# Graph layers on one core: one buffer per layer for the summed messages in place of two, every accumulating scatter behind the landing of the one before it

## The reference

```python
def _gin_layer(x, ei, ea, p, concat):
    enc_w, enc_b, w1, b1, g, be, rm, rv, w2, b2 = p
    ee = ea @ enc_w + enc_b
    src = x[ei[1]]
    h = jnp.concatenate([src, ee], axis=1) if concat else src + ee
    agg = jax.ops.segment_sum(h, ei[0], num_segments=x.shape[0])
    h = agg @ w1 + b1
    h = jax.nn.relu(_bn_eval(h, g, be, rm, rv))
    return h @ w2 + b2
```

## Time and profile before

| what | value |
|---|---|
| median of 3 runs | 15496.48 us (15484.17 to 15514.05) |
| span of the profiled execution, first to last instruction | 13500.7 us |
| the profiled execution's own time | not given apart from its span |
| busy, share of the span | PE 56%, weight loads 40%, DVE 47%, ACT 31%, POOL 55% |
| mean granted clock of TensorE | 0.730 |
| gathers L637 | 784 of one form, 811.0 us, 1034 ns each (392 more read the first layer's input) |
| scatters L649 | 1176, 1847.8 us, 1571 ns each |
| adds of the two buffers L1341 | 588, 417.0 us, 713 ns each |
| loads of the sum buffers L435 | 1176, of 256 KB (784) and 290 KB (392) |
| stores of zeros L398 | 1182, of 256 KB (788) and 290 KB (394) |
| read from and written to HBM | 882.49 and 989.71 MB |

### The profile page before, as it was taken

How to read it: one execution, slowest core, us unless ns; L and a number is a source line. 1 busy time by engine, 2 the same in 40 slices (tenths; PEclk the granted TensorE clock), 3 DMA queues, 4 the chain that set the end, 5 groups by cost and what they waited for, 6 DMA issues and landing times.

```text
span 13500.7 us, 178567 instructions
## 1 busy us (share of the span) xinstructions
PE 7584.9 (56%) x35409; PEld 5358.3 (40%) x35409; DVE 6400.1 (47%) x28822; ACT 4190.8 (31%) x8872; POOL 7379.7 (55%) x6837
## 2 busy tenths in 40 slices
PE   6777555555555555554222488842228993222888
PEld 3333444434444333433212355631225662222565
DVE  6777666667666677775222344411113331111444
ACT  7999311111111222221000255510004550000443
POOL 4444677777777777777777400057770007776000
PEclk9999666666666666665555799965559995555999
DMA  6777931138111652222333455533226772223988
GB/s 230 265 266 266 347 131 46 46 104 293 47 47 47 219 208 69 69 69 57 45 45 45 110 192 196 195 70 40 40 40 207 232 231 41 40 40 57 273 268 259
DMA packets 1765076, 1853.43 MB, mean 137 GB/s; under 512 B 232093, under 2 KB 1250168, under 8 KB 1764794
## 3 DMA queue, kind: packets, MB, share of 16 engines
q1 hardware_dynamic: 1424418, 1430.53, 32.1%
q0 software_dynamic: 332416, 418.41, 15.4%
q10 hardware_dynamic: 7960, 2.01, 0.1%
HBM read 882.49 MB, written 989.71 MB: 139 GB/s over the span
## 4 chain that ended last, share of the span: by engine, by line
issue 16%; POOL 11%; DMA 10%; PE 8%; SPq 5%; DVE 3%; POOLq 1%; DVEq 0%; ACT 0%; ACTq 0%
DMA bXd<-agg_d 8%; POOL bO L637 6%; POOL agg_d L649 5%; PE ps L991 3%; SPq L435 2%; PE ps L978 2%; DMA agg_d<-dO,dOI 2%; SPq L433 2%; DVE aO L1368 1%; PE ps L968 1%; DVE bXd L1341 1%; PE ps L940 1%; PE ps L979 1%; DVE eE L1362 1%; SPq L438 0%
## 5 line engine op out<-in xcount | busy, mean ns | idle before, releaser
L637 POOL DMA_INDIRECT bO<-g_d,dGI x784 | 811.0, 1034 | 2486.2 <-DMA g_d<-aH 2242.2
L649 POOL DMA_INDIRECT agg_d<-dO,dOI x1176 | 1847.8, 1571 | 473.8 <-issue 376.2
L949 PE MATMUL ps<-bO,bNE 128*128 128x128 f32 (+1 forms) x2352 | 836.0, 470 | 1569.4 <-DMA bO<-g_d,dGI 1040.7
L767 ACT COPY dO<-ps 128x128 f32<-128x128 f32 (+1 forms) x1176 | 319.3, 272 | 3550.6 <-DMA agg_d<-dO,dOI 3497.6
L949 PEld LDWEIGHTS ps<-bO,bNE 128*128 128x128 f32 x2352 | 563.7, 305 | 1825.0 <-issue 1793.3
L978 PE MATMUL ps<-aS,W1X 128*128 128x512 f32 x2352 | 1207.9, 594 | 5.8 <-DMA eET<-eaT_d 5.3
L991 PE MATMUL ps<-W,aT 128*128 128x128 f32 x9408 | 1133.4, 280 | 27.9 <-ACT aS L784 27.9
L891 PE MATMUL ps<-ident,bSB 128*128 128x128 f32 x1176 | 288.0, 425 | 1522.6 <-DVE bSB L1194 1522.6
L991 PEld LDWEIGHTS ps<-W,aT 128*128 128x128 f32 x9408 | 1102.3, 196 | 48.0 <-ACT aS L784 46.8
L790 ACT ACTIVATE aT<-ps,BNT,BNS 128x512 f32<-128x512 f32 x1176 | 911.2, 775 | 654.2 <-PE ps L979 628.0
L1376 DVE TENSOR_TENSOR aH<-ps,B 128x512 f32<-128x512 f32 x588 | 406.7, 692 | 1252.2 <-PE ps L991 1252.2
(11 more groups left out here) (188 smaller groups left out, 19624.4 us busy)
## 6 DMA issues: line engine op xcount, KB each, us to landing
agg_d<-zeros SPq DMA_DIRECT2D x788, 256.0 KB
bXd<-agg_d SPq DMA_DIRECT2D x784, 256.0 KB, 4.4
agg_d<-zeros SPq DMA_DIRECT2D x394, 290.0 KB
bXd<-agg_d SPq DMA_DIRECT2D x392, 290.0 KB, 4.1
yg_d<-aYG SPq DMA_DIRECT2D x196, 512.0 KB, 3.0
aX<-yg_d SPq DMA_DIRECT2D x392, 256.0 KB, 4.0
g_d<-aH SPq DMA_DIRECT2D x392, 256.0 KB, 3.7
aX<-g_d SPq DMA_DIRECT2D x392, 256.0 KB, 3.8
```

The source lines that it names most:

```text
L637: pool.indirect_dma_start(dG[:, u, 0:C], None, gin_in[m], bass.IndirectOffsetOnAxis(ap=dGI[:, u:u + 1], axis=0), bounds_check=lim2 if m == ...
L649: pool.indirect_dma_start(agg_d[m][u % 2], bass.IndirectOffsetOnAxis(ap=dOI[:, u:u + 1], axis=0), dO[:, u, 0:AW[m]], None, bounds_check=ag ...
L949: pe.matmul(ps[2 + u % 4][:, 0:AW[m]], dS[:, u, :], dG[:, u, 0:AW[m]], start=True, stop=True).then_inc(d_acc, 1)
```

## The change

Each layer keeps one sum buffer. All scatters go to it and count up one semaphore `d_a`; each waits until all scatters ahead of it have landed. SP clears one buffer per layer, loads one in the dense stage, and VectorE reads it directly. The target of e_in's count falls from 48 to 32.

```diff
-    agg_d = [[dram(f"agg{m}{b}_d", (NR, AW[m])) for b in range(2)] for m in range(M)]
+    agg_d = [dram(f"agg{m}_d", (NR, AW[m])) for m in range(M)]
...
             for m in range(M):
-                for b in range(2):
-                    agg = agg_d[m][b]
-                    n = J * AW[m]
-                    sp.wait_ge(b_fm, m * R + 1)
-                    with sp.Fori(0, NT + 1) as i:
-                        sp.dma_start(agg[bass.ds(i * TN, TN), :].rearrange("(p j) c -> p (j c)", j=J),
-                                     zeros[:, 0:n]).then_inc(s_zero, 16)
+                n = J * AW[m]
+                sp.wait_ge(b_fm, m * R + 1)
+                with sp.Fori(0, NT + 1) as i:
+                    sp.dma_start(agg_d[m][bass.ds(i * TN, TN), :].rearrange("(p j) c -> p (j c)", j=J),
+                                 zeros[:, 0:n]).then_inc(s_zero, 16)
...
-                    for b in range(2):
-                        sp.dma_start(eA[:, k, b, :, 0:AW[m]], pick(agg_d[m][b])).then_inc(e_in[k], 16)
+                    sp.dma_start(eA[:, k, :, 0:AW[m]], pick(agg_d[m])).then_inc(e_in[k], 16)
...
                     pool.wait_ge(d_o, U * r + u + 1)
-                    if not isinstance(r, int) or U * r + u >= 2:
-                        pool.wait_ge(d_a[u % 2], 16 * ((U // 2) * r + u // 2))
+                    if not isinstance(r, int) or U * r + u >= 1:
+                        pool.wait_ge(d_a, 16 * (U * r + u))
                     pool.sem_inc(s_gate, 1)
-                    pool.indirect_dma_start(agg_d[m][u % 2],
+                    pool.indirect_dma_start(agg_d[m],
                                             bass.IndirectOffsetOnAxis(ap=dOI[:, u:u + 1], axis=0),
                                             dO[:, u, 0:AW[m]], None, bounds_check=agg_last,
-                                            oob_is_err=True, compute_op=ALU.add).then_inc(d_a[u % 2], 16)
+                                            oob_is_err=True, compute_op=ALU.add).then_inc(d_a, 16)
...
                         if not isinstance(r, int) or r > 0:
-                            act.wait_ge(d_a[u % 2], 16 * ((U // 2) * (r - 1) + u // 2 + 1))
+                            act.wait_ge(d_a, 16 * (U * (r - 1) + u + 1))
                         act.copy(dO[:, u, 0:AW[m]], ps[2 + u % 4][:, 0:AW[m]]).then_inc(d_o, 1)
...
                 def add_up(p, m=m, n0=n0):
-                    for k in range(2):
-                        v.wait_ge(e_in[k], 48 * (m * NA + p + 1))
-                        v.tensor_tensor(eA[:, k, 0, :, 0:AW[m]], eA[:, k, 0, :, 0:AW[m]], eA[:, k, 1, :, 0:AW[m]],
-                                        ALU.add).then_inc(e_a, 1)
                     if m == 0:
-                        v.wait_ge(e_a, 2 * p + 2)
+                        for k in range(2):
+                            v.wait_ge(e_in[k], 32 * (p + 1))
...
                     for k in range(2):
-                        v.wait_ge(e_a, n0 + 2 * p + k + 1)
+                        v.wait_ge(e_in[k], 32 * (m * NA + p + 1))
                         if not isinstance(p, int):
                             v.wait_ge(e_tp, n0 + 2 * p + k - 1)
-                        v.tensor_tensor(eS[:, k, :, :], eA[:, k, 0, :, 0:C], eG[:, k, :, :], ALU.add
+                        v.tensor_tensor(eS[:, k, :, :], eA[:, k, :, 0:C], eG[:, k, :, :], ALU.add
                                         ).then_inc(e_s, 1)
```

More of the change, by code:

```diff
@@ L253, in gnn_program @@
         d_c = sem("d_c")
-        e_a = sem("e_a")
         dG = bO
@@ L263, in gnn_program @@
         d_g = sems("d_g", U)
-        d_a = sems("d_a", 2)
+        d_a = sem("d_a")
         d_at, d_k, d_gi, d_oi, d_t, d_s, d_acc, d_o = [
@@ L270, in gnn_program @@
         eY = aX[:, 2:4, :, :]
-        eA = bXd_flat[:, 0:4 * J * (C + EA)].rearrange("p (k b j c) -> p k b j c", k=2, b=2, j=J)
+        eA = bXd_flat[:, 0:2 * J * (C + EA)].rearrange("p (k j c) -> p k j c", k=2, j=J)
         eS = aO[:, 0, :, :, :]
@@ L470, in e_pair @@
                             load_ea(k, 2 * p + 2 + k)
-                for b in range(2):
-                    sp.wait_ge(d_a[b], 16 * (U // 2) * R * (m + 1))
+                sp.wait_ge(d_a, 16 * U * R * (m + 1))
                 if m == 0:
-                    sp.wait_ge(s_zero, 16 * 2 * M * (NT + 1))
+                    sp.wait_ge(s_zero, 16 * M * (NT + 1))
                 else:
@@ L624, in _ @@
             agg_last = pool.to_reg(NR - 1)
-            pool.wait_ge(s_zero, 16 * 2 * M * (NT + 1))
+            pool.wait_ge(s_zero, 16 * M * (NT + 1))
             for m in range(M):
@@ L1325, in d_round @@
                     if not isinstance(r, int) or r > 0:
-                        for b in range(2):
-                            v.wait_ge(d_a[b], 16 * (U // 2) * r)
+                        v.wait_ge(d_a, 16 * U * r)
                     v.sem_inc(s_gate, 1)
@@ L1354, in add_up @@
                         for k in range(2):
-                            ins = v.tensor_tensor(eQ[:, 0, k * J:(k + 1) * J, :], eA[:, k, 0, :, C:C + EA],
+                            ins = v.tensor_tensor(eQ[:, 0, k * J:(k + 1) * J, :], eA[:, k, :, C:C + EA],
                                                   self_ea[:, :, :], ALU.add)
```

## The result

The changed kernel takes 16,404.4 us (16,391 to 16,420) against 15,492.8 of the kernel before: ratio 1.0588, 95% interval 1.0573 to 1.0603, +912 us. It is slower, as forecast, and 261 us quicker than the 16,665 forecast.

The account below looks back on a forecast made before the run. GpSimd was taken to bound the scatter stages; in the dense stages TensorE is busy 82 to 91%. Scatters +1504, dense stages -330 and clearing -5 gave +1169 on 15,496: 16,665 us, range 16,400 to 17,000.

Parts of the forecast that it names:

- The scatters: Scatter stages: each scatter waits for the last one's landing, 4.17 us per dependent pair; +1504 us in sum.
- Nothing else gets a new wait, so nothing hides the added time: Scatter stages: GpSimd is the chain; the 7.2 us from last scatter to next round's first stays.
- The dense stages: One load of two and the adds removed, TensorE's waits shrink: -160, -70 and -100, sum -330 us.
- the bound: Dense stages: the saving lies between 0 and -361 us, from TensorE's waits for VectorE's sum.
- The removed 2.1 us exceed every wait: Dense stages: 2.1 us or more removed per pair against waits of at most 1.8; TensorE should become the bound.
- rival 2: Dense stages give nothing back, as another wait steps in; 16,995 us, chance 0.08.
- The clearing: Half the stores of zeros beside the attention rounds removed: -5 us in the third layer, nothing in the first two.
- I take what lies around the span as unchanged: The timed median's 1995.8 us above the profile's span of 13500.7 was added to the forecast as a constant.
- Rival 1: Whole kernel: timed runs are slower all through by 1.148, so +1169 counts as +1342; 16,838 us, chance 0.14.
- Rivals 3 and 4: Scatter stages: dependent pair only 3.7 or 3.4 us, chance 0.09; wait hides behind gather, 2.9 us, 15,360 us, chance 0.02.

Follow-up runs that it names:

- e2: Kernel before with only the scatter side changed: all scatters to one buffer, each behind the last, both buffers still cleared, loaded and added; 17,221.3 us, ratio 1.0968.
- e10: Kernel before with its two buffers in turn, but every scatter waits for the landing of the one before; 14,977.8 us, ratio 1.1092.
- e6: Changed kernel with LAG = 0, so every scatter on GpSimd stands between two gathers; 16,091.5 us, ratio to before 1.0386.
- e3: Kernel before with only the dense side changed: both buffers scattered to and cleared, one loaded, nothing added; 15,222.2 us, ratio 0.969.
- e8: Kernel before, both buffers and adds kept, rows loaded two pairs ahead into a second set of tiles; 15,176.8 us, ratio 0.9803.
- e9: Kernel before with one buffer loaded in the dense stage but the add kept (wrong sums); 13,192.6 us, ratio 0.9769.
- e11: Kernel before with two buffers, loads two pairs ahead, and the adds moved from VectorE to GpSimd; 13,173.5 us, ratio 0.9751.
- e7: Kernel before with both buffers loaded in the dense stage but not added; 15,279.3 us, ratio 0.9868.
- e12: Changed kernel, no edit, on a chip with quick attention rounds; 14,536.3 us against 13,516.3 of the kernel before, ratio 1.0757.
- e5: Changed kernel again, no edit, on one chip with the kernel before; 16,442.2 us, ratio 1.0616.
- e1: Kernel before, no edit, profiled once more; 15,705.8 us.

## Why the prediction was right, and where not

The direction and the mechanism were right. That the time lies inside the range is partly luck: 16,404 is 4 us above its lower end, and that end was built from an interval of 4.0 us and -361 in the dense stages, where the runs have 4.14 to 4.3, -482, and a clearing of -63 or more. By its terms:

- **The scatters: right.** +1504 was forecast, the two profiles give +1484, e2 +1526. Dependent pairs stand 4.05 to 4.48 us apart on average of a place in the round, most at 4.1 to 4.2 in the second and third layers and at 4.2 to 4.4 in the first; 4.17 was taken from two scatters that waited two apart. e10 shows that the wait is the cause, e6 that the chain of landings is what the round consists of.
- **"Nothing else gets a new wait, so nothing hides the added time": right.** The 7.2 us of four gathers stayed in all three layers.
- **The dense stages: right in kind, too small in size, and past the bound given.** -330 was forecast with -361 as the end, -482 came. The step that failed is the bound: it took TensorE's idle time ahead of the waiting transposes for the whole cost of the wait, and TensorE's busy time (1026.5, 902.1 and 915.1 us) for what remains. In the windows TensorE's idle time fell by 350.6 us, close to the bound's 361; its busy time, with the same instructions, fell to 974.5, 862.9 and 874.8 us, by 131.5, for which the forecast had nothing. Two things are in these 131.5. The first shows in TensorE's timeline around one wait of 0.32 us, of before and then of the changed kernel without it:

```profile
10606.72 0.38 PE L979 MATMUL ps<-eET,EPS 102*128 102x512 bf16 x1
10607.41 1.26 PE L968 MATMUL ps<-ident,aO 128*128 128x128 f32 x8 [0.32 <-DVE aO L1368]
10608.50 3.74 PE L991 MATMUL ps<-W,aT 128*128 128x128 f32 x32
10612.08 1.02 PE L978 MATMUL ps<-aS,W1X 128*128 128x512 f32 x2
```

```profile
13207.55 0.38 PE L974 MATMUL ps<-eET,EPS 102*128 102x512 bf16 x1
13207.77 1.04 PE L963 MATMUL ps<-ident,aO 128*128 128x128 f32 x8
13208.64 3.74 PE L986 MATMUL ps<-W,aT 128*128 128x128 f32 x32
13212.22 1.02 PE L973 MATMUL ps<-aS,W1X 128*128 128x512 f32 x2
```

  The stretch shrinks from 5.36 to 4.67 us, by 0.69 for a wait shown as 0.32: the eight transposes start 0.47 us sooner behind the matmul ahead of them and take 0.22 us less, as TensorE works on without a break. The granted clock is 1.00 in both.

  The second is the clock. In the dense stages of before there are 33 short stretches (21, 3 and 9, the first 40 us of each stage left out; 119 us in sum) with a granted clock of 0.50, that is 1.2 GHz, and 31 of them begin at or close behind a wait of TensorE's of 1.9 to 3.0 us. One of them as a window, TensorE's timeline in it, and the same transposes 12 us later at full clock:

```profile
7770.34:7773.75 3.41, 3.32 (x16) 3.30 (x17) 0.64 (x2) 1.07 (x2) 0.00 (x0) 0.50 0.51 153
```

```profile
7770.43 1.09 PE L966 MATMUL ps<-ident,eE 128*102 128x128 f32 x4 [2.30 <-DVE aO L1368]
7771.32 1.06 PE L968 MATMUL ps<-ident,aO 128*128 128x128 f32 x4
...
7782.92 0.65 PE L966 MATMUL ps<-ident,eE 128*102 128x128 f32 x4 [1.06 <-DVE aO L1368]
7783.40 0.60 PE L968 MATMUL ps<-ident,aO 128*128 128x128 f32 x4
```

  Four transposes take 0.89 us from start to start in place of 0.48. TensorE is busy for 117 us of these stretches, and one transpose follows the other after 213 ns in place of 109, so an estimate from these rows is 117 x (1 - 109/213) = 57 us of the 131.5. The changed kernel has no such stretch, nor have e3, e8, e9 and e11: the mean clock of its first dense stage is 0.99 in place of 0.96.
- **"The removed 2.1 us exceed every wait": right.** TensorE is the bound in all three, with two waits a stage left; rival 2 is out. e7, e8 and e9 show that load and add each counted; only in the second stage was the load alone nearly enough (111 us of 114).
- **The clearing: too small for the timed runs.** -5 was forecast as a profile with quick rounds showed it, and e12 has 6 to 8. On the chip where the rounds are slow it is 63 to 72 us by e5 to e8; 89 is what the result leaves over. I had written that in the first two layers GpSimd covers it; that holds where the rounds are quick (31.6 to 31.7 us with either clearing), and not where they are slow.
- **"I take what lies around the span as unchanged": wrong in its reason.** Nothing of the 1,996 us lies around the span; the profile and the timed runs had attention rounds of different length, and e1's attention stage is 2,193 us longer than the profile's. It did little harm, since the change hardly touches that stage. Rival 1, that everything is slower by 1.148, is out: scatter and dense stages last as long on all four chips.
- Rivals 3 and 4 are out: no place in the round has an average under 4.05 us.

Of the 261 us between forecast and result, -20 are from the scatters and -152 from the dense stages, as the two profiles have them. The clearing adds -58 to -67 by e5 to e8. Some 20 to 30 us are left; the dense stages of before differ by 19 us from profile to profile, and no more can be said of them.

## What to carry to other kernels

A wait for a DMA's landing costs its start-to-start distance, which a profile often holds already where the same kernel waits two apart: here 4.15 us against 1.9 to 3.3 of issue. When a wait in front of TensorE goes, more can come back than the idle time listed, as its busy time shrinks as well (here 351 us idle and 132 busy): look for stretches of low clock behind the waits. And before two buffers are merged for the sake of their loads, load earlier: two pairs ahead gave 313 us with both buffers kept, where merging them cost 912 to 1,020.

## What the runs showed that I had not expected

- The attention rounds take 31.7 us (first two layers, outside the clearing) on some chips and 43 to 45 on others, with the same instructions and, but for TensorE, the same busy time; many of the gaps end in "remote" and "issue". A profile and a timed run of one kernel can come from different chips: compare span and time first. The cause stays open.
- While GpSimd adds 128x580 elements (8302.26 to 8303.83 in e11), VectorE's cast of 128x136, which takes 0.23 us a microsecond earlier, takes 1.32 and ends at 8303.92, with GpSimd's add. The Trainium skill, SBUF — State Buffer, section Who interferes with whom, says that casts can take a port pair that GpSimd shares, and that whoever issues first keeps it for the whole instruction; this row agrees. VectorE's adds of two tiles are longer as well: those of the node's own rows take 0.88 us on average in e11's first dense stage, against 0.69 in e8's.
- In the third dense stage the DMA engines are at 0.98 busy and 289 GB/s in e8 (290 in e11), where TensorE was the bound in the changed kernel at 0.83 and 249.
